# The row sum of a LayerNorm moved from VectorE to ScalarE in a macaron layer on eight cores

## The reference

```python
def _layernorm(x, axis=-1, eps=1e-5):
    m = jnp.mean(x, axis=axis, keepdims=True)
    v = jnp.var(x, axis=axis, keepdims=True)
    return (x - m) / jnp.sqrt(v + eps)

# FFN: a mixture of 8 low-rank maps (rank 64)
h = jax.nn.relu(jnp.einsum('bsd,de->bse', x, W1) + b1)
alpha = jax.nn.softmax(jnp.einsum('bse,ek->bsk', h, W2) + b2, axis=-1)
vx = jnp.einsum('krd,bsd->bskr', V, x)
uvx = jnp.einsum('kdr,bskr->bskd', U, vx)
out = jnp.einsum('bsk,bskd->bsd', alpha, uvx)

# attention: 16 heads of 128, mask open where |block_i - block_j| <= 2, blocks of 64
# the layer
x = x + 0.5 * ffn(_layernorm(x))
x = x + attn(_layernorm(x))
x = x + 0.5 * ffn(_layernorm(x))
```

## Time and profile before

| | us |
|---|---|
| median of 3 timed runs | 3689.4 |
| the three timed runs | 3576.04, 3689.4, 3735.0 |
| the profiled execution | 3482.89 |
| its span on the slowest core (core 1) | 3481.2 |
| spans of the eight cores | 3436.4 to 3481.2 |

### The profile page before, as it was taken

The page is one execution under the profiler, slowest core; times in us unless marked ns, Lnnn a source line. Parts: engine busy times, 40 slices in busy tenths (PEclk is TensorE's granted clock), DMA queues, the critical chain, the costliest instruction groups (busy, mean ns, idle before and its releaser), DMA issues. The chain is left out here.

```text
span 3481.2 us, 35496 instructions; the slowest of 8 cores (3436.4 to 3481.2 us)
## 1 busy us (share of the span) xinstructions
PE 2383.8 (68%) x12236; PEld 1142.1 (33%) x12236; DVE 1069.8 (31%) x2178; ACT 620.7 (18%) x1234; POOL 78.5 (2%) x77
## 2 busy tenths in 40 slices
PE   2684748768677697376726956487686876973757
PEld 1342324333333243232213423243332433432322
DVE  5102442412503315601352024414124032156013
ACT  2111021311202113211021100213112121132110
POOL 0000000000000000000000000000000000000000
PEclk9797868889788798688858978688897987976888
DMA  4343123033051320144252331120320413200442
GB/s 134 37 49 49 16 34 49 1 49 49 1 73 25 49 49 1 13 60 55 92 157 37 49 49 22 28 49 1 53 45 6 68 25 49 49 1 13 61 72 98
DMA packets 136158, 157.56 MB, mean 45 GB/s; under 512 B 2332, under 2 KB 125232, under 8 KB 131376
## 3 DMA queue, kind: packets, MB, share of 16 engines
q0 software_dynamic: 130320, 117.48, 23.8%
q1 hardware_dynamic: 5664, 37.81, 2.9%
HBM read 255.98 MB, written 16.78 MB: 78 GB/s over the span
## 5 line engine op out<-in xcount | busy, mean ns | idle before, releaser
L513 PE MATMUL pg<-XnT,wSA 128*128 128x512 bf16 (+1 forms) x1536 | 316.2, 372 | 123.1 <-DMA wSA<-wk 116.4
L692 PE MATMUL pg<-wSB,aoAll 128*128 128x512 bf16 x1024 | 281.9, 424 | 49.2 <-DVE Xb L699 38.6
L356 PE MATMUL pg<-XnT,wSB 128*128 128x512 bf16 (+1 forms) x1280 | 263.2, 365 | 75.0 <-DMA wSB<-w 74.5
L528 PE MATMUL pg<-wSA,XnT 128*128 128x512 bf16 x1280 | 309.0, 400 | 0.0
L356 PE MATMUL pg<-XnT,wSA 128*128 128x512 bf16 (+1 forms) x1280 | 276.7, 377 | 11.8 <-DVE XnT L270 11.2
L513 PEld LDWEIGHTS pg<-XnT,wSA 128*128 128x128 bf16 x1536 | 159.5, 105 | 277.9 <-issue 169.6
L320 DVE TENSOR_TENSOR lgacc<-lgacc,plg 128x8 f32<-128x8 f32 x288 | 46.8, 162 | 617.4 <-PE plg L313 617.4
L542 PE MATMUL pg<-XnT,wSB 128*128 128x512 bf16 x1024 | 222.3, 379 | 0.0
L265 PE MATMUL pT<-idb,Xn 128*128 128x128 bf16 x576 | 60.2, 288 | 235.1 <-DVE Xn L255 235.1
L603 ACT ACTIVATE Praw<-pS,att 128x384 f32<-128x384 f32 x256 | 148.8, 581 | 391.7 <-DVE att L593 375.3
L699 DVE TENSOR_TENSOR Xb<-Xb,pg 128x512 f32<-128x512 f32 x256 | 175.9, 687 | 122.1 <-PE pg L692 117.1
(11 more groups left out here) (71 smaller groups left out, 2057.3 us busy)
## 6 DMA issues: line engine op xcount, KB each, us to landing
Xb<-x SPq DMA_DIRECT2D x20, 1024.0 KB, 24.3
wSA<-w POOLq DMA_DIRECT2D x16, 1024.0 KB, 11.2
wSB<-w POOLq DMA_DIRECT2D x16, 1024.0 KB, 11.2
wSA<-wk POOLq DMA_DIRECT2D x8, 2048.0 KB, 17.9
wSB<-wq POOLq DMA_DIRECT2D x8, 2048.0 KB, 28.3
wSA<-wv POOLq DMA_DIRECT2D x8, 2048.0 KB, 15.0
wSB<-wo POOLq DMA_DIRECT2D x8, 2048.0 KB, 14.1
y<-Xb SPq DMA_DIRECT2D x16, 1024.0 KB, 4.0
```

What stands on the lines that cost most here:

```text
L356: t0=t0, nt=nt: e.matmul(bank[:, 0:nt * 128], slot[:, cc * 256 + s4 * 128: cc * 256 + (s4 + 1) * 128], xnt_rhs(t0, nt, cc), start=(cc == 0 ...
L513: e.matmul(bank[:, 0:nt * 128], wS[0][:, cc * 512 + h * 128: cc * 512 + (h + 1) * 128], xnt_rhs(i0, nt, cc), start=(cc == 0), stop=(cc == ...
L528: p.op("tensor", lambda e, bank=bank, l=l, cc=cc: e.matmul(bank[:, :], XnTS(l, cc), wS[0][:, cc * 512:(cc + 1) * 512], start=(cc == 0), st ...
L692: e.matmul(wbank[:, :], aoAll[:, slot * 512 + h2 * 128: slot * 512 + (h2 + 1) * 128], wS[1][:, h2 * D + cg * 512: h2 * D + (cg + 1) * 512] ...
```

## The change

The row sum of each tile is no longer a VectorE `tensor_scalar` (times 1.0, plus 0.0, with `accum_out`), but a ScalarE activation `Copy` with `accum_out`, written to the same column `sl(0, l)` and with the same sink. It stands on ScalarE's list directly ahead of the sum of squares, and signals the semaphore `s_st` as that one does. All else is the same; behind the place the line numbers are one higher (L234 becomes L235, and so on). It applies to all 56 tiles.

```diff
--- before.py
+++ after.py
@@ -229,8 +229,9 @@
             if wait_dx:
                 p.wait("scalar", dxv[(c, l)][0], dxv[(c, l)][1])
                 p.wait("vector", dxv[(c, l)][0], dxv[(c, l)][1])
-            p.op("vector", lambda e, l=l: e.tensor_scalar(
-                sink2, XS(l), 1.0, 0.0, ALU.mult, ALU.add, accum_out=sl(0, l)))
+            p.op("scalar", lambda e, l=l: e.activation(
+                sink2, XS(l), AF.Copy, accum_out=sl(0, l)), inc=s_st)
+            p.wait("scalar", s_st)
             p.op("scalar", lambda e, l=l: e.activation(
                 sink, XS(l), AF.Square, accum_out=sl(1, l)), inc=s_st)
             p.wait("vector", s_st)
```

## The result

| | before | changed |
|---|---|---|
| median of the timed runs | 3531.9 us (10 runs, 3474.31 to 3753.47) | 3422.32 us (10 runs, 3406.29 to 3731.77) |
| ratio, with 95% interval | | 0.9814 [0.9788, 0.9839] |
| profiled execution | 3482.89 us | 3412.91 us |
| its spans, eight cores | 3436.4 to 3481.2 us | 3377.4 to 3411.4 us |

The kernel became 1.86% faster [1.61, 2.12]. The forecast was 1.7% less, and 3418.9 us against the profiled execution's own time; but the time that I put down, 3625 us with a range from 3470 to 3690, was far too high. Some executions of either kernel take several per cent longer than the others, with a lower TensorE clock on one die; the ratios leave them out, and the median of the three runs from which I set out, 6% above the lowest of ten, counts among them.

The account below looks back on a forecast made before the run. VectorE's instruction list was taken to bound the LayerNorm tiles; savings of 14.7, 3.3 and 14.0 us, twice each, made 64.0 us, so 3482.9 became 3418.9 on the profile and 3689.4 became 3625 us, range 3470 to 3690.

Parts of the forecast that it names:

- The sum: Savings of LN1 14.7, LN2 3.3 and LN3 14.0 us, twice each: 64.0 us off the kernel.
- VectorE's 2.40 us a tile: Row sum leaving VectorE's tile loop: 8.84 to 6.44 us in LN1 and LN3, 10.0 to 7.6 in LN2.
- The cover of 0.5 us: In LN1 and LN3, ScalarE's 5.91 us with two passes stays hidden behind VectorE's 6.44 us a tile.
- The first tile: At each stage's start the added pass is uncovered: LN1 and LN2 start 2.10 us later, LN3 loses 0.4.
- Tiles behind a piece: Tile 4 in LN1 and LN3, and tile 8 in LN1, gain nothing: their transposes queue behind TensorE's piece.
- LN2: Tiles 1 to 3 and 7 gain 2.40 us each, 4 and 8 lose 2.10, 5 and 6 neither; 3.3 us a stage.
- rival B: TensorE's clock rises too, in transposes and pieces: 38 us more, 102 in all; chance 0.14.
- C: ScalarE becomes the bound, its pass 3.38 us and loop 7.19: only 32 us saved; chance 0.10.
- D: Copy needs another ScalarE table, three more loads of 1.283 us per tile: about 108 us slower; chance 0.04.
- E: Stages shorten but the time returns in weight waits or TensorE's clock: no gain, 3483 or 3689 us; chance 0.06.
- Two side sums: A 6.9 us ScalarE pass makes the loop 10.7 us; a 2.66 us table switch would double the 108 us loss.

Follow-up runs that it names:

- the run with two passes: The changed kernel with the ScalarE row sum done twice per tile; ratio to before 1.0031 [1.0009, 1.0052].
- the early version: The changed kernel with each stage's first sum on VectorE and LN2's tile 4 emitted before the first K piece, last tile drained sooner; ratio to before 0.9756.
- LN2's alone: The kernel before, with the row sum moved to ScalarE only in LN2 (20 of 56 tiles); ratio to before 1.0011 [0.9992, 1.0029].
- the hybrid: The changed kernel with the sum back on VectorE at each stage's first tile and LN2's tiles 4 and 8; ratio to before 0.9781.

## Why the prediction was right or wrong

**The number.** The sum against the profiled execution was 3418.9 us; the profiled execution of the changed kernel took 3412.91, the median 3422.32, 48 us below the lower end of the range. The step that failed is the one that carried the saving over to the median of the three runs shown, "3689.4 - 64.0 = 3625 us", and the range that was "mostly the spread of the timed runs". The profiled execution, 3482.89 us, lay below all three, and I noted that no row told why, yet took the higher level. Seven further runs of the kernel before put its lowest at 3474.31 and its median over ten at 3531.9. The ratio that the same sum gives, 0.9826 of 3689.4 or 0.9816 of 3482.9, is inside the measured interval. Of the three chances, "the same" (within 2%) had 0.55 and is the nearest; the interval reaches over 2%.

**VectorE's 2.40 us a tile** held: 8.84 fell to 6.43 and 10.0 to 7.6 to 7.8.

**The cover of 0.5 us** held, by the row of the read that ends at 41.60 and by the run with two passes at 8.01 us.

**The first tile** held: 9.69 to 11.79, 2.10 us later; in LN2 2.02. In LN3 the 0.4 us of loss did not come: 11.85 before, 11.78 now.

**Tiles behind a piece.** Tiles 4 and 8 in LN1, put down as no gain, gained 0.40 and 0.28, and tile 5, put down as 2.40, 2.56. Tile 9, put down as 2.40, gained 0.86: this was misread. ScalarE of the changed kernel there, the ReLU of piece 3 and the last square root:

```profile
85.75 0.69 ACT L370 ACTIVATE h_s<-pg,b1T 128x512 bf16<-128x512 f32 x1 [3.66 <-PE pg L357]
86.53 0.20 ACT L249 ACTIVATE stats<-stats 128x1 f32<-128x1 f32 x1
```

and VectorE over the same time, the last small instruction and the reciprocal:

```profile
84.52 0.15 DVE L242 TENSOR_SCALAR stats<-stats 128x1 f32<-128x1 f32 x1
86.91 0.16 DVE L253 RECIPROCAL stats<-stats 128x1 f32<-128x1 f32 x1 [2.23 <-ACT stats L249]
```

The last tile's square root is emitted by `drain`, behind the ReLU of piece 3, so it waits for that piece's matmuls. The wait for VectorE had turned into one for TensorE. The errors of single tiles, up to 1.5 us, nearly cancel: LN1 13.8 for 14.7, LN3 14.5 for 14.0. So the sum is good to about a microsecond a stage, and that the six stages came to 63.9 us for 64.0 is luck.

**LN2.** Tiles 1 to 3 and 7 gained 2.59, 2.24, 2.40 and 2.40; tiles 4 and 8 lost 1.43 and 1.64 where I had 2.10 each; tiles 5 and 6 lost 0.2 and 0.3 where I had none. The smaller loss of tiles 4 and 8 goes with the K piece that stands ahead of them: in the mean over cores and chunks piece 0 took 5.37 us instead of 6.15 and piece 4 5.56 instead of 6.11, a trace of rival B; what raised the clock there is not shown. ScalarE at tile 4 of the changed kernel:

```profile
447.05 0.59 ACT L520 CAST Kb<-pg 128x512 bf16<-128x512 f32 x1 [11.64 <-PE pg L514]
...
447.73 1.91 ACT L232 ACTIVATE Qb<-Xb 128x2048 bf16<-128x2048 f32 x1
...
449.82 1.91 ACT L235 ACTIVATE Qb<-Xb 128x2048 bf16<-128x2048 f32 x1
```

and VectorE's first small instruction of that tile:

```profile
452.00 0.15 DVE L238 TENSOR_SCALAR stats<-stats 128x1 f32<-128x1 f32 x1 [10.50 <-ACT Qb L235]
```

From eviction to small instructions it is 452.00 - 447.05 = 4.95 us, 5.0 forecast, and VectorE's wait grew from 6.98 to 10.50 us. At tile 5 its wait for the square root grew from 1.67 to 4.24 us, by about what its list had lost: a gain that found no taker, as foreseen. The reciprocal of tile 5 in the changed kernel:

```profile
464.93 0.16 DVE L253 RECIPROCAL stats<-stats 128x1 f32<-128x1 f32 x1 [4.24 <-ACT stats L249]
```

**The rivals.** B did not come in (1.87 us for steady transposes; only the two K pieces above were faster), nor C (1.910 us for the pass), D (six table loads) or E (the rest of the span grew by 3.7 us of 2837, less than it differs between profiles of these kernels).

**Two side sums were off**, without effect on the forecast. With a ScalarE pass of 6.9 us the loop would be 5.91 - 1.91 + 6.9 = 10.9 us, not 10.7. And a switch at twice the price would more than double the loss of D: a steady tile would lose 5.91 + 6 x 1.283 - 8.84 = 4.8 us and not 0.9. No row shows such a price. Where a load stands between two instructions of the changed kernel, the second starts 580.50 - 579.14 = 1.36 us after the first ends, about half of the 2.66 us that the prediction names:

```profile
578.55 0.59 ACT L534 CAST Vt<-pg 128x512 bf16<-128x512 f32 x1 [4.23 <-PE pg L529]
579.21 1.28 ACT L604 ACT_TABLE_LOAD   x1
580.50 0.58 ACT L604 ACTIVATE Praw<-pS,att 128x384 f32<-128x384 f32 x1
```

**The rule** of the Trainium skill that additions belong on VectorE (ScalarE: Activation LUTs, Rules for kernel authors) does not decide here: the row has 1.910 us on ScalarE against 2.29 on VectorE for this float32 pass, and the engine with time to spare was ScalarE, for one pass. The two-pass run shows where that ends.

## What to carry to other kernels

When work moves from the engine that sets a loop to one beside it, work out the second engine's loop from the same rows: here 5.91 us against 6.44, and one pass more turned 1.9% faster into 0.3% slower. Then go through the tiles one by one, in every engine's own order, since the gain exists only where the next wait is for the relieved engine: an instruction queued behind an eviction waits for matmuls, whatever feeds it, and moving it ahead of the eviction brought more (23.5 us a stage of LN2, against the early version) than moving the pass (3.7). And set a forecast against the execution whose rows it is summed from; three timed runs that all lie above it are a reason to doubt the runs' level, not to adopt it.

## What the runs showed of the hardware that was not expected

The part of the span outside the six stages has the same instructions in the same order in every kernel here, yet its mean over the cores was 2832.6 to 2854.8 us, and it does not follow the edits. That is 0.8% of that part, so an effect of 8 us such as LN2's alone is seen in the stages and not in the time. It goes with the granted clock over that part: 0.863 where it is 2832.6 us long, 0.860 where it is 2854.8, and 0.855 in the hybrid's 2853.5. Which of the two moves the other stays open. And 40 small matmuls, the last some 1 us ahead of the transposes, had the clock up for these (1.05 us) but not for the whole piece that began 1.4 us after them (5.12 us).
